# Two graph layers in one kernel: where the cosine envelope and the scatter rows are computed

## The reference, cut to what matters

```python
# layer 0
msg = edge_weight[:, None] * x[src]
agg = segment_sum(msg, dst)
x = layernorm(x + relu((x + agg) @ W1 + b1) @ W2 + b2)
# layer 1
h1 = x @ lin1_w.T
c = 0.5 * (cos(edge_weight * pi / 10) + 1)                 # the envelope
f = softplus(edge_attr @ nn_w1.T + nn_b1) - log(2)
W = (softplus(f @ nn_w2.T + nn_b2) - log(2)) * c[:, None]
agg = segment_sum(W * h1[dst], src)
x = layernorm(x + (h1 + agg) @ lin2_w.T + lin2_b)
```

## Time and profile before

| | us |
|---|---|
| device time, median of 3 (lowest, highest) | 11409.07 (11406.62, 11414.97) |
| span of the profiled execution, first to last instruction | 10525.9 |
| POOL busy in it | 8198.7 (78%) |
| PE busy | 7436.3 (71%) |
| DVE busy | 5192.8 (49%) |
| ACT busy | 3563.9 (34%) |

### The profile page before, as it was taken

How to read it: one execution, slowest core, us unless ns; L and a number is a source line. 1 busy time by engine, 2 the same in 40 slices (tenths; PEclk the granted TensorE clock), 3 DMA queues, 4 the chain that set the end, 5 groups by cost and what they waited for, 6 DMA issues and landing times. The chain is left out here.

```text
span 10525.9 us, 195130 instructions
## 1 busy us (share of the span) xinstructions
PE 7436.3 (71%) x29136; PEld 4988.6 (47%) x29137; DVE 5192.8 (49%) x18098; ACT 3563.9 (34%) x8395; POOL 8198.7 (78%) x6525
## 2 busy tenths in 40 slices
PE   3444444444444444699899988889889888988886
PEld 2333333333333333455555555555555555555554
DVE  4444444444444444644444444444444444444445
ACT  0000000000000000555555555555555555555554
POOL 5777777777777777388888888888888888888884
PEclk9999999999999999766666666666666666666765
DMA  4333333333333333466566666666666666666566
GB/s 127 82 82 83 82 82 82 82 83 83 82 82 82 82 82 72 141 92 91 92 91 92 92 91 91 92 92 91 92 91 92 91 92 92 91 92 91 92 91 183
DMA packets 1182378, 971.23 MB, mean 92 GB/s; under 512 B 241395, under 2 KB 1057154, under 8 KB 1181856
## 3 DMA queue, kind: packets, MB, share of 16 engines
q0 software_dynamic: 571152, 430.07, 30.6%
q1 hardware_dynamic: 557384, 515.54, 18.4%
q10 hardware_dynamic: 53832, 25.53, 1.0%
HBM read 706.92 MB, written 263.45 MB: 92 GB/s over the span
## 5 line engine op out<-in xcount | busy, mean ns | idle before, releaser
L996 POOL DMA_INDIRECT sum_table<-rows,sidx x3232 | 4996.6, 1546 | 1010.0 <-issue 787.8
L320 POOL DMA_INDIRECT xg<-x_rows,gidx x3224 | 3117.5, 967 | 1047.5 <-issue 842.0
L343 PE MATMUL bank<-onehot,xg 128*128 128x64 f32 x6448 | 1907.8, 439 | 2266.6 <-DMA xg<-x_rows,gidx 1244.1
L343 PEld LDWEIGHTS bank<-onehot,xg 128*128 128x128 f32 x6448 | 1532.7, 318 | 2641.2 <-DMA xg<-x_rows,gidx 1086.2
L859 PE MATMUL bank<-filt,same 128*128 128x128 f32 x6464 | 1379.0, 383 | 641.4 <-DVE filt L1045 637.7
L859 PEld LDWEIGHTS bank<-filt,same 128*128 128x128 f32 x6464 | 1235.8, 285 | 713.1 <-DVE filt L1045 590.3
L302 ACT ACTIVATE gidx<-srcf 128x4 int32 x806 | 165.6, 205 | 3949.6 <-DMA xg<-x_rows,gidx 3935.4
L850 PE MATMUL bank<-w_nn2T,hid 128*128 128x128 f32 x6456 | 1357.3, 376 | 0.0
L830 PE MATMUL bank<-attr,nn 51*128 51x512 f32 x1612 | 1329.5, 918 | 2.4 <-DMA attr<-attr_cols 2.3
L850 PEld LDWEIGHTS bank<-w_nn2T,hid 128*128 128x128 f32 x6456 | 1155.5, 269 | 278.9 <-issue 278.9
L1042 DVE SCALAR_TENSOR_TENSOR filt<-bank,soft 128x512 f32<-128x512 f32 x807 | 556.9, 690 | 1479.6 <-ACT soft L904 1476.5
(11 more groups left out here) (116 smaller groups left out, 4642.9 us busy)
## 6 DMA issues: line engine op xcount, KB each, us to landing
srcb<-src SPq DMA_DIRECT2D x1612, 128.0 KB, 3.0
dstb<-dst SPq DMA_DIRECT2D x806, 128.0 KB
attr<-attr_cols SPq DMA_DIRECT2D x806, 102.0 KB
sum_table<-rows,sidx POOLq DMA_INDIRECT x3232, 4.2
xg<-x_rows,gidx POOLq DMA_INDIRECT x3224, 2.7
h1w<-h_parts SPq DMA_DIRECT2D x806, 32.0 KB
f_tab<-sum_table SPq DMA_DIRECT2D x100, 256.0 KB, 3.9
sum_table<-zero ACTq DMA_DIRECT2D x1209, 16.5 KB
```

The costliest lines, as they stand in the source:

```text
L320: pool.indirect_dma_start(xg[s][:, :], None, x_rows, bass.IndirectOffsetOnAxis(ap=gidx[s // HALF][:, s % HALF:s % HALF + 1], axis=0),).the ...
L343: nc.tensor.matmul(bank[h][:, 0:WIN], xg[s][:, :], onehot[h][:, s % HALF, :], start=(s % HALF == 0), stop=(s % HALF == HALF - 1)).then_inc ...
L996: pool.indirect_dma_start(tabs[s], bass.IndirectOffsetOnAxis(ap=sidx[h][:, s:s + 1], axis=0), rows[h][:, s * P:s * P + P], None, compute_o ...
```

## The change

The envelope is computed in the setup: DVE takes the three steps of the argument at the end of its list, ACT takes absolute value, sine and square behind its last step. The counts are no longer kept: in the loop of layer 0 DVE computes the scatter rows of the tile itself, with three instructions in place of L389. The loads of `base` and `nwin` are put ahead of the stores of the 16-bit rows on SP's queue, the bias split goes to the front of DVE's list and its nine transfers from SP to POOL. Between the layers POOL keeps only the transfers that start the semaphores; they are now eight indirect ones, four plain writes and four additions of zeros into the spare rows.

```diff
@@ setup, sync
+                    sp.wait_ge(win_st, 16 * 2 * NGRP)
+                    sp.dma_start(base[:, 0:T], ...).then_inc(s_tab, 16)
+                    sp.dma_start(nwin[:, 0:T], ...).then_inc(s_tab, 16)
                     for i in range(NGRP):
                         sp.wait_ge(dst_half, i + 1)
                         sp.dma_start(dst16[...], rows_h[0:g[i], i, 0, :]).then_inc(s_st, 16)
...
-                    sp.wait_ge(s_split, 5)
-                    for i, n in enumerate(("b2", "nnb2", "lin2b")):
-                        for k in range(3):
-                            sp.dma_start(bias3[n][k:k + 1, :], ...).then_inc(s_b3, 16)
@@ setup, scalar
+                    act.wait_ge(s_pool, 11)
+                    act.wait_ge(turns_done, 3)
+                    nc.scalar.activation(envelope[:, :], envelope[:, :], ACT.Abs).then_inc(env_steps, 1)
+                    act.wait_ge(env_steps, 1)
+                    nc.scalar.activation(envelope[:, :], envelope[:, :], ACT.Sin, bias=half_pi[:, 0:1],
+                                         scale=-PI / (2 * CUTOFF)).then_inc(env_steps, 1)
+                    act.wait_ge(env_steps, 2)
+                    nc.scalar.activation(envelope[:, :], envelope[:, :], ACT.Square).then_inc(env_steps, 1)
+                    act.wait_ge(env_steps, 3)
@@ setup, gpsimd
+                    pool.wait_ge(s_split, 5)
+                    for i, n in enumerate(("b2", "nnb2", "lin2b")):
+                        for k in range(3):
+                            pool.dma_start(bias3[n][k:k + 1, :], ...).then_inc(s_b3, 16)
@@ setup, vector (the bias split moves to the front)
+                    dve.wait_ge(w_in, 16)
+                    dve.tensor_scalar(envelope[:, :], wgt[:, :], 1.0 / (2 * CUTOFF), magic, ALU.mult, ALU.add).then_inc(turns_done, 1)
+                    dve.wait_ge(turns_done, 1)
+                    dve.tensor_scalar(envelope[:, :], envelope[:, :], magic, -2 * CUTOFF, ALU.subtract, ALU.mult).then_inc(turns_done, 1)
+                    dve.wait_ge(turns_done, 2)
+                    dve.tensor_tensor(envelope[:, :], wgt[:, :], envelope[:, :], ALU.add).then_inc(turns_done, 1)
@@ layer 0, edges, vector
                                 dve.wait_ge(scat_set, j + 1)
+                                dve.tensor_scalar(aside[:, :], srcf[:, ds(here, SUB)], spare_row[:, 0:1], -1.0,
+                                                  ALU.subtract, ALU.mult).then_inc(aside_set, 1)
...
-                                dve.tensor_copy(repeats[:, ds(here, SUB)], dup[:, :]).then_inc(scat_set, 1)
+                                dve.wait_ge(aside_set, 2 * j + 1)
+                                dve.scalar_tensor_tensor(aside[:, :], dup[:, :], 0.0, aside[:, :], ALU.is_gt, ALU.mult).then_inc(aside_set, 1)
...
+                                dve.wait_ge(aside_set, 2 * j + 2)
+                                dve.tensor_tensor(scat[:, ds(here, SUB)], aside[:, :], srcf[:, ds(here, SUB)], ALU.add).then_inc(scat_set, 1)
@@ layer 0, nodes, scalar
-            in_turn(act, (3, relu), (1, take_x1T), (2, root), (1, take_h1), before_end=edge_tables)
+            in_turn(act, (3, relu), (1, take_x1T), (2, root), (1, take_h1))
@@ layer 0, nodes, gpsimd
-            (the 16 primes and the eight operations L706 to L721)
+            for k in range(NTAB):
+                pool.indirect_dma_start(tabs[k], bass.IndirectOffsetOnAxis(ap=spare_idx[0:P >> k, 0:1], axis=0),
+                                        zero[0:P >> k, :], None).then_inc(scattered[k], 16)
+            for k in range(NTAB):
+                pool.wait_ge(scattered[k], 16)
+                pool.indirect_dma_start(tabs[k], bass.IndirectOffsetOnAxis(ap=spare_idx[0:P - 32 * k, 0:1], axis=0),
+                                        zero[0:P - 32 * k, :], None, compute_op=ALU.add).then_inc(scattered[k], 16)
```

More of the change, by code:

```diff
@@ L84, in edge_network_kernel @@
         wgt = sb("wgt", [P, T * SUB], f32)
-        repeats = sb("repeats", [P, T * SUB], f32)
+        envelope = sb("envelope", [P, T * SUB], f32)
         scat = sb("scat", [P, T * SUB], i32)
@@ L94, in edge_network_kernel @@
         spare_row = sb("spare_row", [P, 1], f32)
+        spare_idx = sb("spare_idx", [P, 1], i32)
+        half_pi = sb("half_pi", [P, 1], f32)
         eps = sb("eps", [P, 1], f32)
@@ L140, in _ @@
                         sp.dma_start(nwin_d[P * i:P * i + g[i], :], most[0:g[i], i:i + 1]).then_inc(win_st, 16)
+                    sp.wait_ge(win_st, 16 * 2 * NGRP)
+                    sp.dma_start(base[:, 0:T], base_d[0:T, :].rearrange("t o -> o t").broadcast_to([P, T])).then_inc(s_tab, 16)
+                    sp.dma_start(nwin[:, 0:T], nwin_d[0:T, :].rearrange("t o -> o t").broadcast_to([P, T])).then_inc(s_tab, 16)
                     for i in range(NGRP):
@@ L203, in _ @@
                 def _(dve):
+                    dve.wait_ge(s_brow, 48)
+                    hi, mid, lo = (bpart[0:1, k, :, 0, :] for k in range(3))
+                    dve.tensor_copy(hi, brow[:, :, :]).then_inc(s_split, 1)
+                    dve.wait_ge(s_split, 1)
+                    dve.tensor_tensor(brest[:, 0, :, :], brow[:, :, :], hi, ALU.subtract).then_inc(s_split, 1)
+                    dve.wait_ge(s_split, 2)
+                    dve.tensor_copy(mid, brest[:, 0, :, :]).then_inc(s_split, 1)
+                    dve.wait_ge(s_split, 3)
+                    dve.tensor_tensor(lo, brest[:, 0, :, :], mid, ALU.subtract).then_inc(s_split, 1)
+                    dve.wait_ge(s_split, 4)
+                    dve.tensor_copy(bpart[:, :, :, 1:4, :].rearrange("o k i a d -> o (k i) a d"),
+                                    bpart[:, :, :, 0:1, :].rearrange("o k i a d -> o (k i) a d")
+                                    .broadcast_to([1, 9, 3, D])).then_inc(s_split, 1)
                     for i in range(NGRP):
@@ L256, in edge_network_kernel @@
                 rel = sb2("rel", [P, SUB], f32)
+                aside = sb2("aside", [P, SUB], f32)
                 tables_zero, weights_in = sem("tables_zero"), sem("weights_in")
@@ L401, in edge_network_kernel @@
             layer1_edges(nc, sem, lambda n, s, d: c4.enter_context(nc.sbuf_tensor(n, s, d)), src16, dst16, attr_cols,
-                         h1_parts, tabs, srcf, wgt, scat, basef, base, nwin, pidx, spare_row,
+                         h1_parts, tabs, srcf, envelope, scat, basef, base, nwin, pidx, spare_row,
                          ones3, zero, scattered, bias3, nn1, w_sb["nn2T"], bank)
@@ L688, in _ @@
                 act.sem_inc(s, CREDIT)
-            def edge_tables():
-                act.wait_ge(table_steps, 8)
-                nc.scalar.activation(scat[:, :], turns_buf[:, :], ACT.Copy)
-                nc.scalar.activation(u[:, :], u[:, :], ACT.Abs).then_inc(sined, 1)
-                act.wait_ge(sined, 1)
-                nc.scalar.activation(u[:, :], u[:, :], ACT.Sin, bias=half_pi[:, 0:1], scale=-PI / (2 * CUTOFF)).then_inc(sined, 1)
-            in_turn(act, (3, relu), (1, take_x1T), (2, root), (1, take_h1), before_end=edge_tables)
+            in_turn(act, (3, relu), (1, take_x1T), (2, root), (1, take_h1))
```

58 lines of the change are left out of this document (11 added, 47 removed).

## The result

| | before | after | ratio (95% interval) |
|---|---|---|---|
| device time, median of 20 runs each, us | 11406.44 (11391.96 to 11417.25) | 11386.39 (11367.70 to 11397.59) | 0.9983 [0.9977, 0.9989] |

The change makes the kernel 20 us faster where 52 were forecast. The direction is right and the size is not: the median is 29 us above the forecast, though inside its range.

The account below looks back on a forecast made before the run. POOL's gathers and scatters were taken to bound the edge loops, with DVE stalled beside POOL between them. 10525.9 - 57 + 5 + 0 = 10473.9, and 11409.07 - 52 = 11357 us with the rest unchanged; range 11325 to 11402.

Parts of the forecast that it names:

- The rest up to the median: Whole kernel: the 883.2 us between the profiled span, 10525.9, and the timed median, assumed unchanged by the edit.
- 4.16 us of cover on DVE a tile: Layer 0's loop: DVE idles 4.16 us a tile waiting for the last products, so added DVE time costs nothing.
- the change touches nothing there: Layer 1's edges: POOL sets their pace and only the name of the envelope's tile changes, so 0 us.
- The head and the tail of the node block: Between the layers: DVE's stalls beside POOL's long operations go, 44 us; the late wait and multiplication go, 13 us; together -57.
- the new transfers: Node block's head: eight indirect transfers take 12.5 us of POOL, over when L508 first runs; at most 1.5 us if late.
- The setup: Before the first gather: the envelope's DVE and ACT steps end at 63.7 against 59.1 before; +5 us, ends +3 and +9.
- The 1.06 ns a column: Setup: rate taken for DVE's two-input operation on 128 x 3224, giving 3.6 us.
- Layer 0's loop: Three new DVE instructions replace a copy while POOL's gathers set the pace; 0 us, range -25 to +40.
- The comparisons: Layer 0's loop: eight existing DVE comparisons beside gathers whose median stays 947 ns, taken as evidence the new instructions cost nothing.
- rivals B and C: Layer 0's loop: new DVE instructions lengthen gathers, up to 11460, chance 0.10; or gathers get shorter, 11332, chance 0.12.
- Rival D: Node block: some stall stays because POOL's indirect transfers hold DVE up; at most 1.5 us, inside the forecast's chance of 0.62.
- Rival A: Node block: only half of the head's gain comes, 22 us lost to the pipeline's start; 11379 us, chance 0.16.

Follow-up runs that it names:

- e2_env_only: Changed kernel with the scatter rows computed by POOL between the layers and the counts' copy back in layer 0's loop; 0.9985 of before on a quick-loop chip, 0.9953 on a slow-loop one.
- e1_rows_only: Kernel before with only the scatter rows computed per tile on DVE, the envelope still between the layers; 1.0004 of before on a chip with the quick loop.
- c4: The kernel before and the changed kernel, both unmodified, on one chip with the slow loop; 11513.84 and 11440.10 us, ratio 0.9934.
- c4_before: The kernel before, unmodified, traced again on a chip with the slow loop; 11513.84 us in one run.
- c4_after: The changed kernel, unmodified, on the same slow-loop chip as c4_before; 11440.10 us, 0.9934 of before.
- e5_loop_x4: Changed kernel with nine more DVE instructions a tile in layer 0's loop, three of each new kind, results unread; 11574.45 us in one run, against 11511.17 for before.
- e3_pad3: Changed kernel with three small memsets added on POOL ahead of layer 1; 11435.89 us, 0.993 of before on a chip with the slow loop.
- c3_before: The kernel before, unmodified, on the slow-loop chip that also ran e3_pad3 and e5_loop_x4; 11506.31 us in one run.
- e9_pool_one_less: Changed kernel with one setup memset moved from POOL to DVE, so the first scatter is POOL's instruction 122 as before; 10486.08 us, 0.9951 of before.

## Why the prediction was wrong

**The steps that failed** are two. The first is the sentence after the sum: "The rest up to the median, 883.2 us, is taken as unchanged." It is no rest outside the instructions. Every run's time is its span and 1.5 to 2.0 us, and the difference is layer 0's loop, which the page shows at 4107 us and the timed runs of the same kernel had at some 4980. So the loop I costed, at POOL's pace with 4.16 us of cover on DVE a tile, was not the loop that was timed. That the page's span was 8% below the median should have stopped me: a term of 883 us, seventeen times the forecast gain, had no row. In place of the 0 that I had for the loop, the changed kernel's was some 20 us longer on the chip of the result, by the sum below. The second is "the change touches nothing there", of layer 1, put at nothing: it took 17 us more.

**The head and the tail of the node block**, -57, were right in mechanism and somewhat small: -65.6 and -63.0 in the two same-chip pairs. L508's stall is gone and so is the wait behind `edge_tables`. What was mis-sized is the start: I had the wait for `n_xr` unchanged, but DVE's first L731 now waits for PE and not for that load, and comes 5062.47 - 5051.98 = 10.5 us after the last gather in place of 4188.18 - 4171.3 = 16.9. This belongs to the envelope's half: the same distance is 11.4 us in e2_env_only, with DVE waiting for PE, and 17.3 in e1_rows_only, with DVE waiting for the load. The indirect transfers in place of the 16 plain ones are in that half; that they let the load land earlier is likely and was not tested alone. The prediction also had the new transfers over when the first norm runs. They were not; they did not hold it up.

**The setup**, +5: +3.7 and +5.8. Right, with its steps one by one. The 1.06 ns a column of its two-input step does not come out of the earlier trace rows by division (0.69 us for 512 columns is 1.35 ns); it holds as the increment between 256 columns and 512, and the step measured 3.52 us.

**Layer 0's loop**, 0 with -25 to +40: +1.6 on kind Q, where it was worked out. The comparisons were the right nearest row, and rivals B and C, which needed a gather 16 ns longer or a loop 25 us shorter, fell there. On kind S the pair of c4 gives -44 in the traces and some -33 by the medians, outside the bounds.

**Layer 1**, "the change touches nothing there": +17.7 and +16.1. This was wrong. 1542 ns became 1549, 3232 times. Added to the rest on kind Q: 3.7 + 1.6 - 65.6 + 17.7 + 0.1 = -42.5 in the spans, -46 in the medians. That this lies so near the forecast 52 is in part luck: 8.6 us too little in the node block stand against 17.7 missed in layer 1.

**Rival D** fell: L535 takes 1.11 beside an indirect transfer. **Rival A** fell with the head. Two slips in the working change nothing: 967 - 942 is 25 ns and not 24, and the chances of "faster" add up to 0.83, not 0.82.

**From -46 or -74 to -20.** The change is worth 46 us on kind Q, 74 on the S chip of c4_before and c4_after, and 20 on the chip of the result. Leaving the loop out, the stages' differences in the two pairs are on average +5 (setup) - 64 + 17 = -42. To arrive at -20 its loop has to be some 20 us longer there than before's. The medians say the same: 11406.4 - 1.8 - (65.5 + 228 + 5984 + 150) = 4977 us for before, and 11386.4 - 1.8 - (72.5 + 162.8 + 6001.1 + 150.0) = 4998 for after. On that chip the loop of before is some 100 us shorter and the one of after some 40 to 55 shorter than in the other two groups of kind S, so even the slow loop has no one value. I worked this difference out; no trace of before from that chip shows it, and it stays **open** whether the +20 are the new DVE instructions in that chip's loop (30 us at e5_loop_x4's price), the wander that gave -44 and -43 elsewhere, or gathers drawn out: their mean on the changed kernel's page is 972.7 ns, against 966.3 and 965.4 in before's traces of kind S, which is 21 to 24 us. But e3_pad3's mean is 972.2, and its loop was 22 us shorter than c3_before's. Open too is what makes a scatter 7 or 11 ns longer from build to build, and what makes a chip one of kind S.

A version with before's scatters would, by this sum, be some 17 us faster than the changed kernel; the two attempts at it, by the program's place, did not give it (e9_pool_one_less and the changed kernel lie within each other's intervals).

## What to carry to other kernels

Lay the profile's span beside the timed median before anything is costed: where they differ by more than the few microseconds around a launch, the profiled execution ran in another condition, and the stage that differs has to be found before its idle time is used as cover. A long POOL operation beside a pipeline that lives on DVE is worth moving even if POOL has time, since DVE's one-source operations stood still for nearly all of it. And a small gain is measured against every loop of a kernel, not against the edited one alone: 7 ns in an instruction that runs 3232 times took back over a quarter of what the edit brought.

## What the hardware showed unexpectedly

- On some chips sequencer instructions (register arithmetic, moves, loads, waits) took 0.70 us each in bursts, in common steps across DVE, ACT, POOL and SP. The same program's loop then took 5075 to 5084 us in place of 4106, with the instructions of the engines themselves at their usual length (gathers 966 ns on average against 967). Layer 1, where only SP's were slow, did not suffer: it took 5983.6, 5981.9 and 5983.9 us on the two kinds.
- The issue of a scatter by POOL had a length of its own per build: 1542, 1549 or 1553 ns as median, the same on both kinds of chip, independent of its place in the program over six places, in kernels whose layer 1 is the same but for the name of one tile and the numbers of its semaphores.
- DVE's TENSOR_SCALAR of 512 columns in all took 24.86 us beside POOL's tile operations and 1.11 beside POOL's indirect transfers; with four of the seven tile operations left it took 32.51, with three 17.07. What held DVE up was POOL's work on tiles, not its issue of transfers.
